# Attention maxima: the causal mask moves from TensorE products to a VectorE add-and-reduce

## The reference

```
att = jnp.einsum('bhqd,bhkd->bhqk', q, k) / jnp.sqrt(jnp.float32(hd))
att = att + bias.transpose(2, 0, 1)[None]
att = jnp.where(causal[None, None], att, -jnp.inf)
att = jax.nn.softmax(att, axis=-1)
out = jnp.einsum('bhqk,bhkd->bhqd', att, v)
```

## Time and profile before

| what | value |
|---|---|
| median of 3 runs | 1147.46 us (1146.35 to 1148.29) |
| profiled execution, its own time | 1143.46 us |
| span of that execution | 1141.7 us |
| busy in the span | PE 970.5, DVE 948.4, ACT 769.8, POOL 774.8 us |
| L1453, mask products, 128 of 128x256 bf16 | median 273 ns |
| L1599, maxima over 256 columns, 64 times | mean 423 ns |
| L1600, maxima over 512 columns, 64 times | mean 682 ns |

### The profile page before, as it was taken

How to read it: one execution, slowest core, us unless ns; L and a number is a source line. 1 busy time by engine, 2 the same in 40 slices (tenths; PEclk the granted TensorE clock), 3 DMA queues, 4 the chain that set the end, 5 groups by cost and what they waited for, 6 DMA issues and landing times. The chain is left out here.

```text
span 1141.7 us, 25505 instructions
## 1 busy us (share of the span) xinstructions
PE 970.5 (85%) x9849; PEld 514.2 (45%) x9849; DVE 948.4 (83%) x1737; ACT 769.8 (67%) x1690; POOL 774.8 (68%) x425
## 2 busy tenths in 40 slices
PE   5799999999999999999999998871774999998375
PEld 2344444444434444444444444431453666675254
DVE  3599999999999999999999999969891456664995
ACT  4888889889898888897988878813331245544332
POOL 1488988989989889889898898963341123322252
PEclk9999999999999999999999999985786599998788
DMA  6554444435443436353445443307201011000001
GB/s 241 175 181 132 150 133 149 149 105 199 128 150 131 149 115 197 121 168 125 139 140 158 123 159 115 130 1 158 31 1 19 1 20 20 13 9 2 0 1 38
DMA packets 65420, 119.17 MB, mean 104 GB/s; under 512 B 40004, under 2 KB 46980, under 8 KB 56324
## 3 DMA queue, kind: packets, MB, share of 16 engines
q1 hardware_dynamic: 65300, 117.54, 33.1%
HBM read 109.13 MB, written 6.29 MB: 101 GB/s over the span
## 5 line engine op out<-in xcount | busy, mean ns | idle before, releaser
L845 POOL TENSOR_TENSOR prod<-hid,c_rep 128x1024 f32<-128x1024 f32 x256 | 612.8, 2428 | 97.0 <-DVE hid L778 96.9
L778 DVE TENSOR_TENSOR_SCAN hid<-decay,acc 128x256 f32<-128x256 f32 x1024 | 609.9, 664 | 37.4 <-PE acc L498 33.9
L682 ACT ACTIVATE decay<-delta,a_neg 128x255 f32<-128x255 f32 x1024 | 428.0, 497 | 60.6 <-DVE hid L778 60.2
L498 PE MATMUL acc<-b_diag,du_t 64*64 64x256 f32 x4096 | 273.9, 383 | 35.5 <-DVE hid L778 35.5
L521 PE MATMUL ring<-prod,ident 64*64 64x512 f32 x2048 | 245.2, 594 | 4.4 <-POOL prod L845 3.8
L498 PEld LDWEIGHTS acc<-b_diag,du_t 64*64 64x64 f32 x4096 | 145.9, 133 | 199.5 <-issue 114.5
L1661 POOL TENSOR_SCALAR_AFFINE_SELECT att_probs<-att_probs 128x512 f32<-128x512 f32 x64 | 40.6, 634 | 133.2 <-ACT att_probs L1705 133.2
L521 PEld LDWEIGHTS ring<-prod,ident 64*64 64x64 f32 x2048 | 78.2, 134 | 103.2 <-issue 82.2
L1705 ACT ACTIVATE att_probs<-acc 128x384 f32<-128x384 f32 x128 | 55.8, 488 | 78.9 <-PE acc L1472 78.9
L413 PE MATMUL ring<-xpad,diag_cw 64*64 64x512 f32 x512 | 60.5, 589 | 1.0 <-ACT xpad L606 0.9
L1470 PE MATMUL acc<-att_qk 17*128 17x256 f32 x256 | 56.6, 460 | 0.5 <-ACT att_probs L1705 0.4
(11 more groups left out here) (166 smaller groups left out, 1349.5 us busy)
## 6 DMA issues: line engine op xcount, KB each, us to landing
c_rep<-c_rows SPq DMA_DIRECT2D x64, 1024.0 KB, 4.8
b_diag<-diag_rows SPq DMA_DIRECT2D x64, 512.0 KB, 3.8
diag_rows<-prod SPq DMA_DIRECT2D x2, 2048.0 KB, 10.6
att_qk<-in_pos_q SPq DMA_DIRECT2D x4, 768.0 KB
att_qk<-att_dense SPq DMA_DIRECT2D x32, 64.0 KB
att_qk<-in_pos_k SPq DMA_DIRECT2D x4, 288.0 KB
resid<-in_x SPq DMA_DIRECT2D x4, 256.0 KB, 3.1
c_rows<-bc SPq DMA_DIRECT2D x64, 8.0 KB, 1.5
```

Of the source, the lines that this page charges most:

```text
L498: last = nc.tensor.matmul(inj[m * HALF:(m + 1) * HALF, K % 2, at:at + HALF * SG], du_t[rows, n % 2, e, chans:chans + HALF], b_diag[rows, K ...
L682: last = nc.scalar.activation(decay[:, K % DECAYS, s, 1:], delta[:, n % 2, h, e * SEQ + 1:(e + 1) * SEQ], ACT.Exp, scale=a_neg[:, lay(n) % ...
L778: last = nc.vector.tensor_tensor_scan(hid[:, K % HIDS, s, :], decay[:, K % DECAYS, s, :], rows[:, s, :], 0.0, ALU.mult, ALU.add)
L845: nc.gpsimd.tensor_tensor(prod[:, K // 4 % 2, h, :, at], hid[:, K % HIDS, :, :], c_rep[:, g, :, at], ALU.mult).then_inc(s_prod, 1)
```

## The change

The mask products on TensorE are gone, the score products begin their own accumulation, and the two reductions of `peaks` become four instructions, one for each head and query tile. Each adds the mask to the scores, multiplies by -1, writes the 128 or 256 results to a new SBUF tile `masked`, and gives their minimum, which is the negated maximum, as one number a partition. The mask lies in a tile `masks` with 128 columns of zeros in front, in float32; `masked` has four buffers.

```
-        ident_b = sb("ident_b", [P, P], BF16)
-        mask_b = sb("mask_b", [P, 2, P], BF16)
+        masks = sb("masks", [P, 2 * P])
+        masked = sb("masked", [P, 4, SPAN])
...
-                def mask_scores(u):
-                    banks.wait_free(t, "s", u)
-                    for i in range(2):
-                        nc.tensor.matmul(diagonal(score_bank(u)[:, i:i + 1, 0:SPAN])[:, 0], ident_b[:, :], mask_b[:, :, :],
-                                         start=True, stop=False, skip_group_check=True)
...
-                        return nc.tensor.matmul(out[:, 0:P], q[:, 0:P], k[:, 0:P], start=False, stop=True, skip_group_check=True)
-                    return nc.tensor.matmul(out[:, P:SPAN], q[:, P:], k, start=False, stop=True, skip_group_check=True)
+                        return nc.tensor.matmul(out[:, 0:P], q[:, 0:P], k[:, 0:P], start=True, stop=True)
+                    return nc.tensor.matmul(out[:, P:SPAN], q[:, P:], k, start=True, stop=True)
...
-                        mask_scores(s)
+                        banks.wait_free(t, "s", s)
...
-                t.wait_ge(s_maskb, 2)
...
-                    g, at = u // 2, slice(js[0] * STRIP + MAX_ROW, js[1] * STRIP + MAX_ROW + 1, STRIP)
+                    g, js = u // 2, where(u)[2]
...
-                    nc.vector.tensor_reduce(npk[:, g % 2, 0, at], score_bank(u)[:, :, 0:P], AX, ALU.max, negate=True)
-                    last = nc.vector.tensor_reduce(npk[:, g % 2, 1, at], score_bank(u)[:, :, P:SPAN], AX, ALU.max, negate=True)
+                    for i in range(2):
+                        for c, (cols, hidden) in enumerate(((slice(0, P), masks[:, P:]), (slice(P, SPAN), masks[:, :]))):
+                            scores, col = score_bank(u)[:, i, cols], js[i] * STRIP + MAX_ROW
+                            last = nc.vector.tensor_tensor_reduce(masked[:, (2 * u + i) % 4, cols], scores, hidden, -1.0, -NEG, ALU.add, ALU.min,
+                                                                  npk[:, g % 2, c, col:col + 1])
                     banks.read(last, "s", u)
...
+                v.wait_ge(s_maskb, 2)
...
-                nc.gpsimd.tensor_copy(ident_b[:, :], ident[:, :]).then_inc(s_maskb, 1)
-                nc.gpsimd.tensor_copy(mask_b[:, :, :], tiles.mask[:, :].unsqueeze(1).broadcast_to([P, 2, P])).then_inc(s_maskb, 1)
+                nc.gpsimd.memset(masks[:, 0:P], 0.0).then_inc(s_maskb, 1)
+                nc.gpsimd.tensor_copy(masks[:, P:], tiles.mask[:, :]).then_inc(s_maskb, 1)
```

## The result

The changed kernel takes 1151.58 us (1145.37 to 1153.61, 20 executions) against 1147.53 us (1142.15 to 1149.27, 20 executions) of the kernel before on the same chip: ratio 1.0038, interval 1.0023 to 1.0054. The forecast was 1143.3, faster. The profiled execution of after took 1147.72 us (span 1146.0); that of before took 1143.46 (span 1141.7).

The account below looks back on a forecast made before the run. TensorE's path of 4.26 us a group was taken as the bound, with VectorE's loop taking over at 4.22; 1.6 us steady plus 2.6 before 918 us saved 4.2, giving 1139.3 profiled and a 1143.3 median, range 1137 to 1160.

Parts of the forecast that it names:

- Bound and path: Attention stage, plain group: TensorE's path through mask pair, scores and exponentials sets 4.26 us; without mask products it would be 3.94.
- The maxima: VectorE: two reductions become four instructions, main parts about 0.29 and 0.42 us, 1.10 a unit before writing the reduced numbers.
- r: VectorE's write of the reduced number after each maxima instruction: forecast 0.074 us, bounds 0 and 0.154.
- E: Time one unit's maxima take on VectorE from start to next start: 0.94 us before, forecast 1.40.
- the pair: Two successive groups, with the moments and then the normalising for the next tokens: 9.11 us before, forecast 9.95.
- Steady sum: The 27 intervals between add_row starts from 918.62 to 1042.87: 1.6 us saved, VectorE setting the plain group at 4.22.
- rival 2: VectorE's write of the reduced number is hidden: E = 1.10, plain group 3.94, total 1135.8 us; chance 0.15.
- Before 918 us: Stretch at the lower clock with eleven mask pairs, six counting whole: 1.9 to 3.2 us saved, 2.6 taken.
- the pair beside the exponentials: TensorE's mask pair after turn_mixed: 0.32 us hidden while ScalarE runs the exponentials, so removing it saves nothing in plain groups.
- rival 4: TensorE's clock rises a group later or falls back, about 2.5 us more for that group: 1145.8 us; chance 0.05.
- rival 1: VectorE's reduced number costs an unoverlapped step: r = 0.154, E = 1.72, plain group 4.86, total 1158.8 us; chance 0.30.

## Why the prediction was wrong

- *Bound and path*: right. Plain groups went from 4.26 to 3.94 and the wait for the exponentials stayed at 1.09 us.
- *The maxima*: the main parts right (286 and 420 ns for 0.29 and 0.42), r mis-sized: 0 against the 0.074 that I took from `BATCH_NORM_AGGREGATE`. That small operation takes 0.074 from start to start; the accumulator read has a row of 83 ns and takes none. So E was 1.10 to 1.12 and not 1.40, VectorE did not become the bound (idle before `add_row` 0.69), and the pair took 8.93 instead of 9.95. Of the Trainium skill, "VectorE: DVE Perf Modes", "Two Vector instructions with no wait between them": the trace agrees that the accumulator is read out by an instruction of its own, 256 rows of it. The prediction took from "The DRAIN you can't avoid" that each part runs to its end, E = 1.72, and called a disagreement. It left out that the same section says that a next operation that is not held starts earlier; 1.11 measured agrees with that, and the main parts overlap as in the earlier trace rows. The advice on the number of operations stands among that page's "Rules for kernel authors".
- *Steady sum*: the forecast had -1.6, rival 2 -9.1. Without the fall after has -7.6 over the last 26 intervals: -3.1, -2.7 and -1.8, the last being 10.4 less the fall. The fall's price is 34.28 - 22.18 = 12.1 us, where 22.18 are the same five intervals in the kernel without mask products, at the upper clock and with VectorE's old maxima; with that estimate 1147.72 would be 1135.6.
- *Before 918 us*: 2.6 us forecast, nothing kept. After is 0.8 ahead at the first `add_row` and gains 1.1 more in four intervals, but the fifth takes 6.52 instead of 4.64, since the rise comes at 922; at the sixth, 923.29 against 923.26, all is given back.
- *The step that failed*: the prediction priced the pair beside the exponentials at nothing because its time is hidden, and rival 4, the clock, at a chance of 0.05 and a price of 2.5 us, with the argument that 0.5 us of wait in each plain group leaves the clock at 1.00. That row says nothing of 0.8 us, which is what the change made of it: with the pair put back into that place after takes 1140.94 us and its trace does not fall. The fall is no matter of one group: it lasts until a rise, which took about 27 us in after, and costs 12.1. What exactly lets the clock fall stays open, the part of the four instructions in it too. Rival 2 with a grown rival 4 is what happened: 0.8 lost up to the sixth `add_row`, 7.6 gained after it, 12.1 lost to the fall, together the 5.3 of the table.
- *The range* held the time by luck: the sign was wrong, and rival 1, which carried nearly all of the slower side, had the wrong mechanism for it. With the right E and a clock that holds, the prediction's own sum is rival 2's 1135.8, outside the range on the other side.

The Trainium skill, page "TensorE: Matmul & The Clock Gate", section "A second HAM failure mode: psum-queue depth-cycling", tells of a kernel whose TensorE idles for moments between groups of products so often that its clock swings between the two levels. The traces here agree in kind (six of eight fall with 0.8 us of it in each group by the estimate, none of six with 0.5), and this rule against the change was not weighed in the prediction.

## What to carry to other kernels

A TensorE instruction that stands in the shadow of another engine costs little time, but it may be what keeps the clock up: before removing one, read how much of each period TensorE is then without products, and price a fall by the whole stretch until the next rise, not by one group. Where only part of such work can go, take the part on the path and leave the hidden part: here that is 1140.94 us, 0.9945 of before, against 1151.38 and 1.0045 on the same chip for removing both. It is a safe choice more than the fastest one: with no mask products and the old maxima, which then leave the mask out, the executions of the highest mean clock took 1131 to 1134. A kernel whose executions fall into groups (1131, 1147, 1183), each with its own mean clock, should be judged by many of them and by the clock of each, not by one trace.

## What the runs showed of the hardware that I had not expected

- The read of VectorE's accumulator shows as 83 ns and takes no time of its own from start to start: 230 of its 256 rows start together with the next instruction, and behind the others the next one begins 0.05 to 2.45 us later, in part for a wait on TensorE; E is 1.10 to 1.12.
- The clock falls within stretches in which the rows show TensorE busy throughout (PE 2.00 of 2.00 at a granted 0.54), with single waits of no more than 0.84 us in the 25 us ahead, and can stay at 0.50 for 128 us with TensorE shown busy for 126.92 us.
- Two products of 128x256 in bf16, 0.32 us in a group of 3.94, decide between never falling in the traces (none of six) and falling in most (six of eight).
- Six products of 128x128 in a row, 2.6 us at the lower clock, were followed by a rise 20 us earlier than in after (902 against 922, one trace).
